# First attention of an eight-layer chain: the products that subtract the maximum on 32 rows each, the two query halves in different rows of TensorE

## What is computed

```
scores = jnp.einsum('bhqd,bhkd->bhqk', qf, kf) * scale
causal = jnp.tril(jnp.ones((s, s), dtype=bool))
scores = jnp.where(causal, scores, jnp.finfo(scores.dtype).min)
probs = jax.nn.softmax(scores, axis=-1)
o = jnp.einsum('bhqk,bhkd->bhqd', probs, v)
```

## Time and profile before

| | us |
|---|---|
| median of 3 runs | 2634.44 |
| lowest and highest | 2632.04, 2639.09 |
| the profiled execution, its own time | 2627.89 |
| its span, first to last instruction | 2626.1 |

### The profile page before, as it was taken

One profiled execution on the slowest core, in us unless ns is written; L12 is line 12 of the kernel. 1 busy time (PEld: TensorE's weight loads), 2 busy tenths in 40 slices (PEclk: granted clock), 3 DMA queues, 4 the chain that ended last, 5 costly groups with the idle time before them and its releaser, 6 DMA issues. The chain is left out here.

```text
span 2626.1 us, 34151 instructions
## 1 busy us (share of the span) xinstructions
PE 2225.0 (85%) x12704; PEld 1310.7 (50%) x12704; DVE 1402.9 (53%) x1949; ACT 1264.4 (48%) x2113; POOL 629.5 (24%) x460
## 2 busy tenths in 40 slices
PE   4989999999999767759999957679999977998847
PEld 3657777777777653324444323234444333443434
DVE  3564555554554254559999654159999631113163
ACT  4545556655565232218888832118888841101330
POOL 1555555665566022400000022100000020001021
PEclk8989999999999888869999958879999998999868
DMA  4870111111110310331121001341121003000000
GB/s 102 260 223 25 53 52 52 56 44 52 52 53 32 109 35 21 107 68 20 20 38 20 2 17 53 125 70 23 28 48 28 2 17 129 0 0 5 14 27 34
DMA packets 78947, 138.97 MB, mean 53 GB/s; under 512 B 30808, under 2 KB 40792, under 8 KB 78832
## 3 DMA queue, kind: packets, MB, share of 16 engines
q1 hardware_dynamic: 78832, 137.40, 18.8%
HBM read 95.95 MB, written 41.03 MB: 52 GB/s over the span
## 5 line engine op out<-in xcount | busy, mean ns | idle before, releaser
L2159 POOL TENSOR_TENSOR l0a_p_low<-yT,l0a_p_high 128x1024 fp32r<-128x1024 f32 (+7 forms) x256 | 385.8, 1535 | 282.6 <-ACT l0a_p_high L2187 282.6
L173 POOL TENSOR_TENSOR applied<-prepared,neghalf 128x2 f32<-128x2 f32 x64 | 58.3, 911 | 1410.6 <-DVE prepared L154 1410.6
L1441 DVE TENSOR_REDUCE l2a_mx<-ps 128x2 f32<-128x1024 f32 x256 | 309.2, 1223 | 78.2 <-PE ps L1315 77.5
L1441 DVE TENSOR_REDUCE l1a_mx<-ps 128x2 f32<-128x1024 f32 x256 | 309.3, 1223 | 51.3 <-PE ps L1315 50.6
L2220 DVE TENSOR_REDUCE l0a_mx<-ps 128x1 f32<-128x512 f32 (+3 forms) x384 | 203.6, 554 | 235.9 <-PE ps L2066 145.0
L1422 ACT ACTIVATE l1a_prob<-ps 128x512 f32<-128x512 f32 x512 | 278.1, 596 | 75.2 <-PE ps L1343 58.6
L1422 ACT ACTIVATE l2a_prob<-ps 128x512 f32<-128x512 f32 x512 | 278.1, 596 | 68.6 <-PE ps L1343 50.6
L2176 ACT ACTIVATE yT<-ps 128x1024 f32<-128x1024 f32 (+7 forms) x256 | 166.2, 649 | 188.4 <-PE ps L2088 125.6
L2187 ACT CAST l0a_p_high<-yT 128x1024 fp32r<-128x1024 f32 (+7 forms) x256 | 172.7, 674 | 7.1
L191 ACT ACTIVATE f<-f,applied 128x512 f32<-128x512 f32 x64 | 48.6, 806 | 250.3 <-POOL applied L176 250.0
L1358 PE MATMUL ps<-l1a_prob,l1a_vext 128*32 128x256 f32 x2048 | 166.4, 405 | 0.0
(11 more groups left out here) (297 smaller groups left out, 4065.3 us busy)
## 6 DMA issues: line engine op xcount, KB each, us to landing
l0a_q<-l0a_q SPq DMA_DIRECT2D x32, 512.0 KB, 3.2
l0q_woh<-in_l0a_wo SPq DMA_DIRECT2D x16, 512.0 KB, 5.3
l0a_q<-f SPq DMA_DIRECT2D x32, 256.0 KB, 4.7
l0a_q<-l0q_q_pe SPq DMA_DIRECT2D x32, 256.0 KB, 3.5
l0a_recip_rows<-l0a_recip_row SPq DMA_DIRECT2D x32, 256.0 KB, 3.3
l0a_o<-l0a_o_pair SPq DMA_DIRECT2D x16, 512.0 KB, 2.8
yT<-l0a_o SPq DMA_DIRECT2D x16, 512.0 KB, 3.2
l1a_q<-l1a_q_parts SPq DMA_DIRECT2D x16, 256.0 KB, 5.3
```

What stands on the lines that cost most here:

```text
L1441: nc.vector.tensor_reduce(mx[:, u % 2, :, p, t, c], banks(("pair", m)), AX.X, ALU.max).then_inc(s_red, 1)
L2159: nc.gpsimd.tensor_tensor(p_low[:, j % 4, P * j:T], prob[:, j % 4, P * j:T], p_high[:, j % 4, P * j:T], ALU.subtract).then_inc(s_pl, 1)
```

## The change

The product with minus the maximum becomes the first of a span (it starts the accumulation, which the first score product did before), and those of a block's two spans are issued one behind the other ahead of all other products of the block. It takes 32 rows instead of 128: rows 0 to 31 of `ones` and `mrow` for the queries below 512, rows 32 to 63 for the others. DVE accordingly writes `mrow` in two instructions, maxima of queries 0 to 511 into rows 0 to 7 and of the others into rows 32 to 39, and the semaphore `s_mrow` counts two a head. The number of products, their columns and the score products themselves stay as they are.

```diff
@@ max_chunk
-                        pe.wait_ge(s_mrow, h)
+                        pe.wait_ge(s_mrow, 2 * h)
@@ scores
                 if j == 0:
-                    pe.wait_ge(s_mrow, h + 1)
+                    pe.wait_ge(s_mrow, 2 * h + 2)
                     if not ready:
                         pe.wait_ge(s_low, h - 1)
+                for lo, hi in spans(j):
+                    rows = slice(32 * (lo // 512), 32 * (lo // 512) + 32)
+                    nc.tensor.matmul(ST[j % 2][:, lo:hi], ones[rows, :], mrow[rows, par, lo:hi], start=True, stop=False)
                 for lo, hi in spans(j):
                     out = ST[j % 2][:, lo:hi]
                     diagonal = lo == P * j
                     keys = slice(j * P, (j + 1) * P)
-                    nc.tensor.matmul(out, k_high[:, keys], q_high[:, par, lo:hi], start=True, stop=False)
+                    nc.tensor.matmul(out, k_high[:, keys], q_high[:, par, lo:hi], start=False, stop=False)
                     nc.tensor.matmul(out, k_high[:, keys], q_low[:, par, lo:hi], start=False, stop=False)
-                    nc.tensor.matmul(out, k_low[:, keys], q_high[:, par, lo:hi], start=False, stop=False)
-                    mm = nc.tensor.matmul(out, ones[:], mrow[:, par, lo:hi], start=False, stop=not diagonal)
+                    mm = nc.tensor.matmul(out, k_low[:, keys], q_high[:, par, lo:hi], start=False, stop=not diagonal)
@@ prepare
-                nc.vector.tensor_tensor(mrow[0:NT, par, :].rearrange("r (t q) -> r t q", t=NT),
-                                        bank(par, NMAX)[0:NT, 0:P].unsqueeze(1).broadcast_to([NT, NT, P]), diag[:],
-                                        ALU.mult).then_inc(s_mrow, 1)
+                for c in range(2):
+                    four = slice(NT // 2 * c, NT // 2 * c + NT // 2)
+                    nc.vector.tensor_tensor(mrow[32 * c:32 * c + NT, par, 512 * c:512 * c + 512].rearrange("r (t q) -> r t q", q=P),
+                                            bank(par, NMAX)[0:NT, 0:P].unsqueeze(1).broadcast_to([NT, NT // 2, P]),
+                                            diag[:, four, :], ALU.mult).then_inc(s_mrow, 1)
```

## The result

The changed kernel takes 2697.4 us (median; 2685.8 to 2702.0) beside 2636.7 us for the kernel before on the same chip: a ratio of 1.0224, with a 95% interval from 1.0192 to 1.0256. It is 61 us slower; 2693 was forecast, and 59 us more.

A forecast was written before the change was run, and what follows sets the result against it. TensorE's sequence was taken to bound the heads: 2.16 us a head added, less 0.33 hidden, gives 1.83, times 32 = 59 us. Added to 2634.4 us that makes 2693 us, within a range of 2664 to 2716.

The forecast's parts named there:

- The bound: In the first attention's heads, TensorE's sequence sets the pace; time added or removed moves the end, except inside a wait.
- The price of a change of shape: Each block of scores goes into 32 rows and back, with loads in the open: 2.16 us a head net of removals.
- In: First product with `ones` starts 0.32 instead of 0.23 us behind the last full product: +0.09 in each block.
- The pair: Two products with `ones` start together; next full load 0.42 us later for 512 columns, 0.37 for 384, 0.31 for 256.
- Out: First score product's load lies in the open, 0.34 instead of 0.23 us: +0.11, or +0.05 to +0.06 in some blocks.
- the hidden part: Block 5's 0.33 us disappear in the wait of the turn of the maxima for DVE, leaving 1.83 us a head.
- Rival 2: The two spans do not run side by side and the shape still changes: 2.47 us a head, 2714 us; chance 0.08.
- the wait at the chunks: Weight loads' 25.8 us wait for DVE's reductions hides nothing, as the waiting and the reduced chunk shift together.
- rival 1: Loads for 32 rows run ahead beside full products: 0.64 us a head gained, 2614 us; chance 0.05.
- rival 3: The load of `ones` is hidden though its product is not: 0.95 us a head lost, 2665 us; chance 0.07.
- rival 4: More gaps pull the clock down in the heads, costing 14 us more: 2707 us; chance 0.03.
- DVE's second write: Writing `mrow` in two instructions takes 1.4 us instead of 1.21, covered by 2.2 us: no cost.

The follow-up runs named there:

- experiment 6: The changed kernel with 64 rows in each product with `ones` (0 to 63, 64 to 127) in place of 32: 2691.7 us, 22.31 us a head.
- experiment 5: The changed kernel with both spans' products on rows 0 to 31, so one follows the other: 2718.6 us, 22.93 us a head.
- Experiments 3 and 4: The changed kernel with 32 rows only in block 5, or only in block 6, all rows elsewhere: 2637.1 and 2648.1 us, 20.43 and 20.82 us a head.
- experiment 1: The changed kernel with all 128 rows in the products with `ones`, keeping the new place and DVE's two writes: 2639.5 us, 20.44 us a head.

## Why the prediction was right

- **The bound.** TensorE's sequence set the pace, and time added in it outside a wait moved the end by as much: 1.89 us a head in the period, 60.8 in the stage, 61 in the median.
- **The price of a change of shape**, taken from other layers' rows. In: 0.32 us from a product of 512 columns, as forecast. The pair: 0.43 for a forecast 0.42, and 0.37 for 384 columns, as forecast. Out: 0.34, as forecast. The sum over the blocks, 1.83 with the hidden part, was 3% short of 1.89. Rows of 48 could stand for rows of 32, since 32 and 64 cost the same (experiment 6).
- **The pair runs side by side** (experiment 5). Rival 2, at 2714 us, is what that kernel gave: 2718.6.
- **The hidden part.** Block 5's price disappeared in the wait of the turn, and the wait at the chunks hid nothing, as argued from what DVE's chains hang on: 25.8 us before and after. Experiments 3 and 4 show the first point by itself.
- **The rivals.** No price for the change of shape (rival 1), and the load of `ones` hidden (rival 3): neither, since the pair's record is 0.50 us long, load and stream together, at a start 0.32 behind the product ahead. Within the pair the second load does run beside the first product. The Trainium skill (TensorE: Matmul & The Clock Gate, Part 3) has weight loads of other row groups pulled ahead of running products; the trace agrees for the pair. Across the change from 128 rows to 32 the load starts only 0.07 us before the modelled end of the product ahead. The Trainium skill (TensorEngine Tiling (Array Packing), Key Properties) has TensorE drained where the tiling mode changes; the trace agrees. The clock (rival 4) stayed at its upper level in the heads.
- **DVE's second write** was put at 1.4 us for the two and at nothing on the path. It took 1.39, and by experiment 1 it costs, together with the new place, 0.04 us a head at most.
- **What was a little off.** From the start of the product ahead of a block to that of the product behind it, in the mean of twenty heads, blocks 0 to 7 grew by 0.17, 0.23, 0.22, 0.20, 0.33, 0.00, 0.40 and 0.34 us; with block 5 hidden, the forecast had 0.16, 0.21, 0.21, 0.23, 0.33, 0, 0.39 and 0.30. The largest miss is block 7: the first score product was taken to cost 0.11 before, as in block 3 of the last head, but behind a product of 512 columns it cost 0.06.

```profile
611.23 0.22 PE L2083 MATMUL ps<-l0a_q_high,l0a_k_high 128*128 128x128 f32 x1
611.29 0.28 PE L2084 MATMUL ps<-l0a_q_low,l0a_k_high 128*128 128x128 f32 x1
```

- **What was read too widely.** Not every change of the stationary shape has the gap. In the trace of the kernel before, the next product usually starts 0.16 us before the modelled end of the one ahead. At 0.07 start all 34 that change from 128 to 64 stationary columns, and 51 of the 52 that change from 48 rows to 128. But of the 252 that change from 66 columns (products with the values) to 128 (scores), 250 start at 0.16, and so do all 8 that change from 128 rows to 96 (as from 2346.38, 0.59 long, to 2346.81). So the gap is shown for parts of 32, 48, 49 and 64 rows and for 32 and 64 columns, and absent for 96 rows and 66 columns. The count also takes away a doubt about and the earlier trace rows: the profile puts the loads at 183.45 and 1355.70 down to a wait for ACT, but every change of their kind starts at the same 0.07 (twice 0.06). And x2 in the timeline does not by itself say that two products start together; for the pairs of 48 and 49 rows their length did.

## What to carry to other kernels

A matrix engine that is full in the profile may still lose to a smaller operand: here two narrow products side by side, between products of all 128 rows, cost more than they saved in every block. Whether several pairs that share one change in and out would pay was not tried. Price the change from a place in the trace where the same change of rows or columns already stands, start to start, and set it against the one product that the pair saves: going in and out costs 0.3 to 0.4 us a block here (experiment 5 over the kernel before, in blocks 0 to 3, where nothing is saved), and the product saved is worth 0.11 to 0.23. And where a cost disappears in a wait, the wait is worth a look of its own: moving one instruction out of it was the only gain found here.

## What the runs showed of the hardware

The price of a change of shape did not depend on whether the narrow products had 32 or 64 rows (22.30 and 22.31 us a head). A product that starts together with its neighbour on other rows is free to the hundredth of a microsecond (0.43 us to the next product for one of 512 columns in block 4 and for two in block 0, 0.66 where the two share their rows). A change between 128 rows and 96, or from 66 stationary columns to 128, showed no gap (next start 0.16 us before the modelled end, as without a change), while one to 64 rows or columns did (0.07). And the third attention took 405.8 to 420.1 us in the nine profiled executions, with a mean clock of 0.97 in the shortest and 0.92 in the longest, in kernels that don't differ there. So single executions of this program can lie 14 us apart for this stage alone, and a head's period was the sharper measure.
